# Three key buffers, three value buffers, one context buffer and key tails read in place, in a gated cross-attention stack of four layers

## What is computed

```
for l in 0..3:
    x = x + tanh(g_xattn[l]) * xattn_l(layernorm(x), ctx, ctx)
    x = x + tanh(g_ffn[l])   * ffn_l(layernorm(x))
```

## Time and profile before

| | |
|---|---|
| median of 3 runs | 2433.03 us (2433.03 to 2433.96) |
| profiled execution, span | 2431.5 us |
| granted clock of TensorE, mean | 0.997 of full speed |
| TensorE busy | 2331.2 us (96%) |
| its weight loads busy | 1578.7 us (65%) |
| VectorE busy | 1274.5 us (52%) |
| ScalarE busy | 1140.6 us (47%) |
| GpSimd busy | 853.3 us (35%) |
| DMA | 39.28 MB in 17462 packets, mean 16 GB/s |

### The profile page before, as it was taken

One profiled execution on the slowest core, in us unless ns is written; L12 is line 12 of the kernel. 1 busy time (PEld: TensorE's weight loads), 2 busy tenths in 40 slices (PEclk: granted clock), 3 DMA queues, 4 the chain that ended last, 5 costly groups with the idle time before them and its releaser, 6 DMA issues.

```text
span 2431.5 us, 56000 instructions
## 1 busy us (share of the span) xinstructions
PE 2331.2 (96%) x23735; PEld 1578.7 (65%) x23735; DVE 1274.5 (52%) x2833; ACT 1140.6 (47%) x1762; POOL 853.3 (35%) x1546
## 2 busy tenths in 40 slices
PE   8999989999999999999999999899999999899999
PEld 5676545777776655577777655467777765457777
DVE  6544776545433567644442467764544346765442
ACT  5545487323345558632225546752333455683211
POOL 1232333434331333334432232334434223334342
PEclk9999999999999999999999999999999999999999
DMA  3200120000000000000000000000000000000000
GB/s 141 91 13 2 35 101 2 1 10 10 10 22 1 13 1 16 2 10 10 10 1 21 1 13 1 13 2 10 10 10 10 13 2 13 2 2 2 1 9 9
DMA packets 17462, 39.28 MB, mean 16 GB/s; under 512 B 1792, under 2 KB 11840, under 8 KB 16192
## 3 DMA queue, kind: packets, MB, share of 16 engines
q1 hardware_dynamic: 17216, 35.71, 4.3%
HBM read 29.78 MB, written 4.19 MB: 14 GB/s over the span
## 4 chain that ended last, share of the span: by engine, by line
PE 79%; ACT 7%; DVE 7%; issue 4%; POOL 2%; DMA 0%; ACTq 0%; POOLq 0%; DVEq 0%
PE P L1501 9%; PE P L1288 5%; PE P L1360 5%; PE P L1385 5%; PE P L1510 5%; PE P L1534 5%; PE P L1502 5%; PE P L1372 4%; PE P L1519 4%; PE P L1278 4%; ACT ET L1659 3%; PE P L1295 3%; PE P L1195 3%; PE P L1140 3%; DVE mx L1911 3%
## 5 line engine op out<-in xcount | busy, mean ns | idle before, releaser
L1911 DVE TENSOR_REDUCE mx<-P 128x8 f32<-128x1232 f32 x256 | 367.3, 1435 | 199.2 <-PE P L1195 119.9
L1501 PE MATMUL P<-Et,w 128*128 128x256 f32 x1024 | 265.4, 382 | 0.1
L1501 PEld LDWEIGHTS P<-Et,w 128*128 128x128 f32 x1024 | 191.5, 190 | 63.2 <-issue 34.5
L1955 DVE SCALAR_TENSOR_TENSOR x<-P,w_first,x 128x512 f32<-128x512 f32 x96 | 71.8, 749 | 277.6 <-PE P L1385 96.8
L1613 ACT ACTIVATE Et<-x,sm 128x256 f32<-128x256 f32 x256 | 138.7, 592 | 138.5 <-POOL sm L906 138.1
L1659 ACT ACTIVATE ET<-P 128x2048 f32<-128x2048 f32 x96 | 180.2, 1877 | 43.3 <-PE P L1278 39.9
L1737 ACT ACTIVATE gu<-P 128x256 f32<-128x256 f32 x128 | 49.1, 384 | 307.1 <-PE P L1502 290.4
L2120 DVE SCALAR_TENSOR_TENSOR gu<-gu,P 128x256 f32<-128x256 f32 x128 | 53.8, 420 | 230.0 <-ACT gu L1737 229.9
L900 POOL TENSOR_SCALAR sm<-mv 128x2 f32<-128x2 f32 x96 | 18.6, 194 | 413.5 <-DVE mv L1906 411.5
L1278 PE MATMUL P<-R,KB 32*128 32x256 f32 (+1 forms) x2560 | 155.3, 379 | 0.0
L1288 PE MATMUL P<-ET,VB 128*32 128x256 f32 x2048 | 143.4, 385 | 11.3 <-ACT ET L1659 5.3
(11 more groups left out here) (287 smaller groups left out, 4971.3 us busy)
## 6 DMA issues: line engine op xcount, KB each, us to landing
kvw<-in_wkv SPq DMA_DIRECT2D x12, 672.0 KB, 4.1
x<-in_x SPq DMA_DIRECT2D x16, 256.0 KB, 2.7
out<-x SPq DMA_DIRECT2D x16, 256.0 KB, 2.1
w<-in_w SPq DMA_DIRECT2D x2, 1024.0 KB, 6.6
w<-in_wexp SPq DMA_DIRECT2D x1, 1028.0 KB, 9.2
w_w<-in_wcon SPq DMA_DIRECT2D x1, 1024.0 KB, 11.4
w_w<-in_m3t SPq DMA_DIRECT2D x1, 1024.0 KB, 7.2
w<-in_w1q SPq DMA_DIRECT2D x1, 1024.0 KB, 10.5
```

The source lines that it names most:

```text
L1501: e.matmul(o, wm[:, c, js], s.xT[:, c, :], start=n == c == 0, stop=False, skip_group_check=True)
L1911: e.tensor_reduce(s.mx[:, i, :, 2 * u:2 * u + 2], quad[:, :, 0:2 * NK].rearrange("p g (a k) -> p g a k", a=2), AX.X, ALU.max).then_inc(q_d, 1)
```

## The change

Keys get three buffers of 160 columns, layer `4*b + l` in `(4*b + l) % 3`, whose columns past 154 are zero; `KT` goes. Values get three buffers: number 0 for layer 0 alone, the others in turn for layers 1 to 3, so the ones are written once at the start and `g_one` goes. The context has one buffer, loaded after the values of layer 3. `st` and `sts` read the tail from `KB`; `sts` issues a product for each `j`, as tiles of 32 by 32. GpSimd's `key` is left in layer 0 and layer 1 only; in layer 1 it makes the mask of the batch from its complement first. `zc` goes, `sm` is halved and `z` takes the place of `mx`. All five lists in `TURN` are new, with the waits and the costs that they were searched with.

```diff
-        ctxT = [sb(f"ctx{i}", [128, 2, NP]) for i in range(2)]
+        ctxT = sb("ctxT", [128, 2, NP])
-        mk = sb("mk", [128, 4, NK], bf16)
+        mk = sb("mk", [128, NK], bf16)
-        KB = [sb(f"KB{i}", [128, 4, NK]) for i in range(2)]
-        KT = [sb(f"KT{i}", [128, 4, 32]) for i in range(2)]
-        VB = [sb(f"VB{i}", [128, 16, 32]) for i in range(2)]
-        VR = [sb(f"VR{i}", [128, 4, 32]) for i in range(2)]
+        KB = [sb(f"KB{i}", [128, 4, NP]) for i in range(3)]
+        VB = [sb(f"VB{i}", [128, 16, 32]) for i in range(3)]
+        VR = [sb(f"VR{i}", [128, 4, 32]) for i in range(3)]
+        def kb(b, l):
+            return KB[(4 * b + l) % 3]
+        def vb(b, l):
+            n = 1 + (3 * b + l - 1) % 2 if l else 0
+            return VB[n], VR[n]
...
# turns(), S0
-                        if 4 * b + l >= 2:
+                        yield "name", "begun"
+                        if 4 * b + l >= 3:
                             for s_ in S[1:]:
-                                yield "after", ("attention", s_.i, 4 * b + l - 2)
-                        yield "name", "free"
+                                yield "after", ("attention", s_.i, 4 * b + l - 3)
                         yield "key", b, l, 0
...
                         yield "name", "key"
-                        yield "need", "free"
+                        yield "need", "begun"
+                        if 3 * b + l >= 3:
+                            n = 3 * b + l - 3
+                            before = 4 * (n // 3) + n % 3 + 1 if l else 4 * (b - 1)
+                            for s_ in S[1:]:
+                                yield "after", ("attention", s_.i, before)
                         yield "val", b, l
...
# parts(), shapes(): costs and tile shapes of sts
-                  "sts": 1451 if name == "sts" and of[2] == 3 else 1113,
+                  "sts": 1563 if name == "sts" and of[2] == 3 else 1225,
-        SHAPES = {"sc": "bb", "s2": "bb", "sts": "dd", "st": "ee", ...
+        SHAPES = {"sc": "bb", "s2": "bb", "sts": "ee", "st": "ee", ...
...
# TURN: every string of digits is replaced (PE 1688 digits in both, POOL 592 and 584)
...
# SyncE
-            load_ctx(1)
...
-                if l == 3 and b < 2:
+                if l == 3 and b < 3:
                     e.wait_ge(p_v0, 4 * b + 4)
-                    load_ctx(b + 2)
+                    load_ctx(b + 1)
...
# GpSimd
-            e.memset(zc[:], 0.0).then_inc(g_const, 1)
-            for i in range(2):
-                e.memset(KT[i][:], 0.0).then_inc(g_const, 1)
+            for K in KB:
+                e.memset(K[:, :, NK:NP], 0.0).then_inc(g_const, 1)
             sums(1, g_const)
+            sums(2, g_const)
             def key(b, l, u):
-                K = KB[l % 2]
+                K = kb(b, l)[:, :, 0:NK]
+                if l:
+                    e.wait_ge(d_mask, 4)
+                    own(e.tensor_scalar(mk[:], onem[:, b, :], -1.0, 1.0, ALU.mult, ALU.add))
                 e.wait_ge(a_k, 5 * b + l + 2)
                 if l == 0:
-                    k = K[:].rearrange("p j k -> p (j k)")
-                    e.tensor_scalar(k, k, 0.0625, None, ALU.mult).then_inc(g_k, 1)
-                elif l == 1:
-                    e.wait_ge(d_mask, 5)
-                    e.tensor_tensor(K[:], K[:], mk[:, b:b + 1, :].broadcast_to([128, 4, NK]), ALU.mult).then_inc(g_k, 1)
-                if l < 2:
-                    e.wait_ge(g_k, C.up(g_k))
-                e.tensor_copy(KT[l % 2][:, :, 0:NK - 128], K[:, :, 128:NK]).then_inc(g_k, 1)
-                C.up(g_k)
-                if l == 2:
-                    for s in S:
-                        e.wait_ge(s.d_o, 2 * (4 * b + 1))
-                    sums(0, g_one)
+                    e.tensor_scalar(K, K, 0.0625, None, ALU.mult).then_inc(g_k, 1)
+                else:
+                    e.tensor_tensor(K, K, mk[:].unsqueeze(1).broadcast_to([128, 4, NK]), ALU.mult).then_inc(g_k, 1)
...
# TensorE, ScalarE, VectorE
-            e.wait_ge(g_const, 12)
+            e.wait_ge(g_const, 16)
...
# TensorE, st
-                K = KT[0]
+                K = kb(b, 0)[:, :, 128:NP]
-                e.wait_ge(g_k, 6 * b + 2)
...
# TensorE, sts
-                K = KT[l % 2][:].rearrange("p (u a) k -> p u (a k)", u=2)
+                K = kb(b, l)[:, :, 128:NP]
-                e.wait_ge(g_k, 6 * b + (2, 4, 5, 6)[l])
...
                 for u in range(2):
-                    o = [banks[g // 2][64 * h:64 * h + 64, 256 * u:256 * u + 256] for g, h in enumerate((0, 1, 1, 0))]
-                    for g in range(4):
-                        e.matmul(o[g], selt[G4[g], 2 * u:2 * u + 2, :].rearrange("p a k -> p (a k)"), s.MT[G4[g], :],
-                                 start=l < 3 and u == 0, stop=False, skip_group_check=True)
-                    for g in range(4):
-                        t = e.matmul(o[g], K[G4[g], u, :], s.QT[G4[g], u, :], start=False, stop=True, skip_group_check=True)
+                    eight = [(g, a, banks[g // 2][G4[2 * h + a], 256 * u:256 * u + 256]) for a in range(2)
+                             for g, h in enumerate((0, 1, 1, 0))]
+                    for g, a, o in eight:
+                        e.matmul(o, selt[G4[g], 2 * u + a, :], s.MT[G4[g], :], start=l < 3 and u == 0, stop=False,
+                                 skip_group_check=True)
+                    for g, a, o in eight:
+                        t = e.matmul(o, K[G4[g], 2 * u + a, :], s.QT[G4[g], u, :], start=False, stop=True,
+                                     skip_group_check=True)
...
# TensorE, pv
-                    if l == 2:
-                        e.wait_ge(g_one, 4 * (b + 1))
...
# ScalarE, key
-                if u == 0 and 4 * b + l >= 2:
+                if u == 0 and 4 * b + l >= 3:
                     for s in S:
-                        e.wait_ge(s.d_o, 2 * (4 * b + l - 1))
+                        e.wait_ge(s.d_o, 2 * (4 * b + l - 2))
...
# VectorE, masks
-                e.tensor_scalar(mk[:].rearrange("p a b -> p (a b)"), m1r, 0, None, ALU.not_equal).then_inc(d_mask, 1)
```

More of the change, by code:

```diff
@@ L143, in build @@
         l_last = sem("l_last")
-        l_ctx = [sem(f"l_ctx{i}") for i in range(2)]
+        l_ctx = sem("l_ctx")
         FIRST = ("first",)
@@ L267, in parts @@
                   "qp": 966 if l == 0 else 1765, "sc": (644, 665, 638, 800)[l], "mt": 111, "st": 1225,
-                  "sts": 1451 if name == "sts" and of[2] == 3 else 1113, "s2": (1105, 1105, 1105, 1540)[l],
+                  "sts": 1563 if name == "sts" and of[2] == 3 else 1225, "s2": (1105, 1105, 1105, 1540)[l],
                   "pv": 2793 if l == 0 else 1930 if u else 909, "out": 3460 if l == 0 else 1760, "up": 1760, "down": 7010, "gate1": 2068, "tl": 145,
@@ L280, in parts @@
                    "h1": 275, "h2": 275, "norm": 985, "no": 580}
-            pool = {"split": 1460 if l == 3 else 1100, "key": 2040 if name == "key" and of[1] == 0 else 1400, "mw": 1650, "norm": 1515, "sq": 960,
+            pool = {"split": 1460 if l == 3 else 1100, "key": 1500, "mw": 1650, "norm": 1515, "sq": 960,
                     "bias": 1500 if name == "bias" and of[2] < 4 else 1230, "hw": 2010, "no": 1205, "nz": 1205}
@@ L285, in parts @@
                    "tsum": "DP", "tern": "D", "raw": "S", "late": "S", "kvw": "s", "store": "S",
-                   "key": "PA" if name == "key" and of[1:] == [0, 0] else "PAG" if name == "key"
-                   else "PA", "val": "PDA" if name == "val" and of[1] == 0 else "PD", "norm": "DGA", "bias": "g",
+                   "key": "PAG" if name == "key" and of[1:] in ([0, 1], [1, 0]) else "PA", "val": "PDA" if name == "val" and of[1] == 0 else "PD", "norm": "DGA", "bias": "g",
                    "split": "G", "no": "dg" if l == 0 else "Da", "nz": "dg", "pv": "Pda" if l == 0 else "P",
@@ L599, in build @@
[L599 to L603, removed]
@@ new lines, in build @@
+            "DVE":
+                "3230323203213230232020320202132103213000312322222310022211231321120332222232003332113300003103102210"
+                "0130303003012121120103010321133331003301033101230200303022310122110220100331213312123010130303323111"
+                "0300013133010212323201213021102022000022001003010002002203312330201213121010111111311011011221220103"
+                "0303313312200133133333333331131132112232322322322222222233223320332020220032230202112203033030110011"
+                "0033022330101030323312120203110310132320122001001313200233220103100213231323103031010112131330030301"
+                "3113002222013203120002021200330020203010320002201102231200323333103333030333033313122300231002113111"
+                "3001311111321111112331331232212221231222122222222121112110202022003220232011220303300310101100033232"
+                "3010100312312332020311003110323001020110022313022303223010133113231230130101013212331030100113003321"
```

(8 more changed lines are left out.)

122 lines of the change are left out of this document (55 added, 67 removed).

## The result

The changed kernel takes 2409.86 us, median of 4 runs (2409.08 to 2411.26), against 2433.03 us (2432.13 to 2433.96) before: a ratio of 0.9904, 95% interval 0.989 to 0.9918.

A forecast was written before the change was run, and what follows sets the result against it. TensorE was taken to bound the kernel, with 238 us idle or filler. Known costs of +6.7 us, +6 after slack, and -14 for the lists gave 2423.5, or 2425 us on the scale of medians; range 2406 to 2446.

The forecast's parts named there:

- the good end of the lists: Best case for the new order strings: a third of TensorE's real idle time recovered, -33 us, giving 2406 us.
- the lists: New order of stages on all engines, expected to recover TensorE idle and filler time: -14 us, called the weakest step.
- the 238: TensorE's idle and filler time together before the change, 238.3 us or 9.8% of the span, mostly in attention stretches.
- the spread of the four batches: Idle plus filler of 42.4 to 45.5 us in the four attention stretches, read as how much orders differ.
- the buffers: Third key and value buffers: freed wait under 1.3 us, taken as nothing; new order nearly as good with two.
- the narrow tiles: TensorE's tail scores of layers 1 to 3 as 32x32 tiles: 0.10 us more in 48 stages, +4.8 us.
- A mean share of slack: About a seventh of the attention stretches is slack (44 of 300), so +6 of the known +6.7 us remains.
- the changes of tile shape: TensorE changes tile shape 993 times instead of 981, at 0.07 us each: +0.8 us.
- The start: More memsets and table writes on GpSimd ahead of the count that TensorE, ScalarE and VectorE await: +1.1 us.
- GpSimd, the masks and the context load: GpSimd saves 6.4 us off the path, masking about 0.65 us each; later context load covered: all worth nothing.
- The clock: TensorE's granted share of 2.4 GHz, 0.99 to 1.00 in the attention stretches, was said not to matter.
- The slower rival: Added TensorE products cost 6 to 7 us, deciding if the order recovers under about 2 us: 2440 us, chance 0.28.

## Why the prediction was right, and where its size was off

**Right: TensorE bounds, and the idle and filler time is what can move.** The work changed by 4.8 us and the idle and filler time by 28.5. The forecast was 8 us of gain and the result is 23.2: it lies in the range because the range reached to the good end of the lists.

**Mis-sized: the lists.** The step was "I take -14 us, some 6% of the 238". The runs show -28.8 us for the order alone (2404.28 against 2433.11), 12% of the 238, close to the good end of -33. The weakness was how it was bounded. I took the spread of the four batches, 3 us, as a measure of what another order is worth. But the four batches had come out of one search with the same structure, with its same gaps at the same kinds of stage; their agreement said that the kernel repeats itself, not that it is near its best. What I looked at in the new strings (who is alone at the end, neighbours of the same stream, distance of the keys) was not what changed either. What changed was which stage stands behind each gap, and that could have been counted beforehand: fillers ahead of anything but scores were 383 of 507 in the old order, and 254 in the new. That those 383 were open to a better order, and the 124 ahead of scores forced by the score banks, is my reading of the counts; no run changes one kind of gap alone.

**Right: the buffers give nothing.** "The new order would have been nearly as good with two buffers" and "no list uses the third buffer" were read off the lists and hold in two runs, 2407.7 us with two key buffers and 2404.3 us with the old kernel whole. They hold to about 2 us: the runs spread by more than that. What was not tried is whether a search under the old conditions would have found this order; the run of the new lists in the old kernel shows only that the old conditions allow it.

**Right at the stage, half hidden in the sum: the narrow tiles.** The 0.10 us a stage was measured as 0.11, with groups of eight running together. The 4.8 us, of which I let six sevenths remain, were 2.5 us in the old order and 4.2 in the new (about 2.8 and 6 at equal granted clock). A mean share of slack was the wrong measure: what remains depends on the order, and in the stage shown above the whole price fell into the gap ahead of the next use of the score banks. The price of the changes of tile shape, 0.8 us, was not tested by itself. The Trainium skill's rule (TensorE: Matmul & The Clock Gate, part 3, "The mechanism"), that a weight load overlaps running matmuls only when its row group differs, does not show as a serial group here: two tiles of one row group are in each group of eight, and eight take 0.30 us like four.

**The start** was sized at 1.1 us and measured as 1.0 us of waiting (5.59 us instead of 4.54), 1.7 us in all when undone. Of the 1.7, 0.7 us is the shorter time of the fillers. The first keys come at 12.43 us, 1.3 later than before.

**GpSimd, the masks and the context load** cost or gave no more than 1 to 2 us. GpSimd lost 853.3 - 844.9 = 8.4 us, where 5 were counted. The masking took 0.34 us, not 0.65, which is 1.2 us over four times. The other 2 us lie in stages that the change doesn't touch, and the kernel with two key buffers, whose GpSimd program is the same, has 847.2.

```profile
L886 POOL TENSOR_SCALAR mk<-onem 128x154 bf16<-128x154 bf16 x4 | 1.3, 336 | 7.6 <-DVE mb L1787 7.6
```

Its operands are two-byte and those of the rows it was priced by are not; that this is why is my reading. No wait of TensorE names the context. The account from before to after is then: order -28.8, tiles +4.2, start +1.0 to +1.7, sum -22.9 to -23.6 us, against -23.2 measured. It closes better than its terms are known. With the old lists all the edits together cost 2.0 us and the tiles alone 2.5, though the start is in the first; at equal clock the tiles under the new lists cost about 6. Both leave room for 1 to 2 us that the other edits give back, which no run separates.

**The clock** "doesn't matter" only while the fillers are there. The attention stretches were granted 0.98 to 1.00 with them and 0.94 to 0.98 without, and the fillers were worth 31 to 40 us.

**The slower rival** asked whether the new order recovers less than 2 us. With the old lists in the changed kernel, where it recovers nothing, the time is 2435.07, 2.0 us above before and not clear of it. The tiles alone are clear of it, at 2.5 us. So the rival's mechanism exists, at 2 to 3 us with the old lists instead of 7, and it never decided.

## What to carry to other kernels

When a change adds buffers and also a new schedule, put the new schedule on the old kernel first: here that was the whole gain, and the edits around it cost 5.6 us. To size what a new order may bring, don't compare repetitions of the old one; sort its gaps by what follows them, and look first at those that no shared resource forces. Filler instructions are neither work nor harmless idle time: subtract them from the busy share before judging it, and mind that they overlap the products behind them. Here the order, not their number, was what could be improved.

## What the runs showed that I had not expected

- The fillers are worth 40 us in the old order and 31 in the new. I had expected them to turn into idle time at about the same total (2430 to 2440 us). With the old lists TensorE's mean granted clock falls only from 0.997 to 0.979 of full speed without them, yet the same products are busy for 41.5 us longer.
- A granted clock of 0.94 over 300 us reads as harmless and isn't. The clock has two levels, 2.4 and 1.2 GHz, so a mean of 0.94 is an eighth of the stretch at the lower one. The group of value products shows it: before, 385 ns each; without fillers 406. The idle time ahead of them, 11.3 us before and 31.2 without, is where the fillers stood.

```profile
L1288 PE MATMUL P<-ET,VB 128*32 128x256 f32 x2048 | 152.9, 406 | 31.2 <-ACT ET L1659 24.8 <-issue 5.5 <-ACT R L1695 0.4
```

- The same 22 fillers took 6.71, 7.01 and 6.30 us at the start of three kernels, by when the clock rose behind them. A comparison of two starts has that much luck in it.
- The changed kernel spends 10.2 us at the lower clock from 255.6 us on, and so does the old kernel with the new lists, from 255.0. TensorE was busy for 9.2 of those 10.2 us in the changed kernel, so by the same halving it loses some 5 us there.
